# A decoder block on one core: cross-attention scores and feature map as two 64-row halves side by side, one more tile of cross weights, and new orders of work

## The reference, cut to what matters

```
v = values.reshape(N, -1, HEADS, HEAD_DIM)      # 16 heads of 16
v, k, q = (_feature_map(x, fm_w, fm_b) for x in (v, k, q))   # [exp(z), exp(-z)], z = x_h @ fm_w.T + fm_b: 32 features a head
scores = jnp.einsum('nqhd,nkhd->nhqk', q, k) / jnp.sqrt(jnp.float32(EMBED))
attn = jax.nn.softmax(scores, axis=-1)          # over 64 context rows
out = jnp.einsum('nhql,nlhd->nqhd', attn, v)
return out.reshape(N, S, HEADS * EXP_DIM) @ fc_w.T + fc_b
```

## Time and profile before

| | us |
|---|---|
| median of 3 runs (509.22, 513.79, 513.8) | 513.79 |
| profiled execution | 509.94 |
| its span | 508.0 |
| PE busy | 456.3 (90%) |
| DVE busy | 377.9 (74%) |
| ACT busy | 299.0 (59%) |
| POOL busy | 127.2 (25%) |

### The profile page before, as it was taken

The page is one execution under the profiler, slowest core; times in us unless marked ns, Lnnn a source line. Parts: engine busy times, 40 slices in busy tenths (PEclk is TensorE's granted clock), DMA queues, the critical chain, the costliest instruction groups (busy, mean ns, idle before and its releaser), DMA issues.

```text
span 508.0 us, 7573 instructions
## 1 busy us (share of the span) xinstructions
PE 456.3 (90%) x2424; PEld 289.7 (57%) x2424; DVE 377.9 (74%) x687; ACT 299.0 (59%) x727; POOL 127.2 (25%) x178
## 2 busy tenths in 40 slices
PE   1698879989799999999799999999799999977885
PEld 1463327446465676657365577656365676556664
DVE  5466676857589988667589988758599976657974
ACT  2457776665478846555468846555568846714531
POOL 2001113102413443013314343012414412112510
PEclk9889999999999999999889999999999999998999
DMA  8862500351610002232720002242621000000001
GB/s 276 280 203 72 180 0 1 93 154 45 224 67 1 0 3 76 73 122 64 249 82 1 2 2 62 74 120 77 217 73 37 8 3 0 21 22 0 2 1 43
DMA packets 22431, 38.46 MB, mean 76 GB/s; under 512 B 2552, under 2 KB 6904, under 8 KB 22264
## 3 DMA queue, kind: packets, MB, share of 16 engines
q1 hardware_dynamic: 22392, 37.97, 23.3%
HBM read 23.28 MB, written 14.68 MB: 75 GB/s over the span
## 4 chain that ended last, share of the span: by engine, by line
PE 69%; DVE 12%; issue 6%; ACT 5%; DMA 5%; SPq 2%; POOL 0%; POOLq 0%; ACTq 0%
PE av_bank L570 17%; PE m_bank L536 8%; PE m_bank L537 7%; PE m_bank L538 7%; PE s_pair L556 7%; PE m_bank L678 5%; DVE nmax L948 5%; DMA q_st<-q_parts 4%; ACT e_sb L770 3%; PE m_bank L703 2%; PE m_bank L690 2%; PE m_bank L739 2%; PE m_bank L587 2%; PE m_bank L728 2%; SPq L495 2%
## 5 line engine op out<-in xcount | busy, mean ns | idle before, releaser
L770 ACT ACTIVATE e_sb<-s_pair,nmax 128x512 f32<-128x512 f32 x256 | 173.1, 687 | 69.9 <-DVE nmax L948 69.6
L948 DVE TENSOR_REDUCE nmax<-s_pair 128x2 f32<-128x1024 f32 x128 | 152.4, 1212 | 27.1 <-PE s_pair L556 26.3
L570 PE MATMUL av_bank<-e_sb,v_sb 128*64 128x512 f32 x512 | 123.9, 604 | 3.4 <-DVE ot_lo L960 1.8
L1197 POOL TENSOR_TENSOR v_sb<-v_sb,rsum 128x256 f32<-128x256 f32 x64 | 39.2, 613 | 228.2 <-DVE rsum L956 218.2
L556 PE MATMUL s_pair<-q_st,k_st 64*128 64x512 f32 x256 | 51.1, 463 | 16.5 <-DMA q_st<-q_parts 9.6
L570 PEld LDWEIGHTS av_bank<-e_sb,v_sb 128*64 128x64 f32 x512 | 31.7, 136 | 57.7 <-issue 47.3
L556 PEld LDWEIGHTS s_pair<-q_st,k_st 64*128 64x128 f32 x256 | 21.3, 187 | 66.5 <-issue 31.1
L770 ACT ACTIVATION_READ_ACCUMULATOR e_sb<-s_pair,nmax 128x1 f32 x256 | 51.9, 203 | 0.0
L536 PE MATMUL m_bank<-wo_hi,ot_hi 128*128 128x256 f32 x120 | 35.0, 292 | 1.5 <-DVE ot_lo L960 1.5
L783 ACT ACTIVATE ot_hi<-av_bank 128x512 fp32r<-128x512 f32 x32 | 19.4, 605 | 27.9 <-PE m_bank L538 14.7
L1224 POOL TENSOR_TENSOR sx<-sx,xrec 128x512 f32<-128x512 f32 x24 | 24.9, 1043 | 36.5 <-DVE xrec L1121 36.5
(11 more groups left out here) (170 smaller groups left out, 869.6 us busy)
## 6 DMA issues: line engine op xcount, KB each, us to landing
q_st<-q_parts SPq DMA_DIRECT2D x32, 256.0 KB, 5.3
k_st<-k_parts SPq DMA_DIRECT2D x32, 256.0 KB, 4.4
k_parts<-qkt_hi SPq DMA_DIRECT2D x14, 256.0 KB
k_parts<-qkt_lo SPq DMA_DIRECT2D x14, 256.0 KB
q_parts<-qkt_hi SPq DMA_DIRECT2D x8, 256.0 KB
q_parts<-qkt_lo SPq DMA_DIRECT2D x8, 256.0 KB
out<-x_sb SPq DMA_DIRECT2D x8, 256.0 KB, 2.1
x_sb<-in_x SPq DMA_DIRECT2D x3, 512.0 KB, 7.7
```

Source lines behind the costliest of these rows:

```text
L570: mm = pe.matmul(av_bank[n % AV_BANKS][64 * par:64 * par + 64, :], v_sb[:, m, 2 * p + par, :], e_sb[:, (4 * q + 2 * i + par) % E_RING, :], ...
L770: act.activation(e_sb[:, g % E_RING, :], s_pair[k // 2][:, k % 2, :], ACT.Exp, bias=nmax[:, g % 8:g % 8 + 1], accum_out=esum[:, q % 4, k:k ...
L948: dve.tensor_reduce(nmax[:, at:at + 2], s_pair[i][:, :, :], AX_X, ALU.max, negate=True)\
L1197: pool.tensor_tensor(v_sb[:, m:m + 2, 2 * p:2 * p + 2, :], v_sb[:, m:m + 2, 2 * p:2 * p + 2, :], rsum[:, q % 4, :].rearrange("p (m h) -> p ...
```

## The change

`xs` and `z` become matmuls of 64 rows: the upper half of the partitions and the lower half each have their own matmul, their own weights and their own bank, alternating. An `xs` unit pair computes 8 such products of 128 columns instead of 4 of 128 rows x 256 columns; `z` computes 12 of 64 rows x 256 columns instead of 12 of 128 rows. Both halves of `xs` and `z` are one PE piece now, which waits for two banks. `kblk` shrinks to two blocks per group, and the heads' order in `vblk` and `wfc` follows. `sx` gets a fourth tile. All slots are laid out anew.

```diff
-X_TILES = 3
+X_TILES = 4
-    ("qk", 0, (1, 1), dict(pe=29, act=30, dve=43, sp=74)),
+    ("qk", 0, (1, 1), dict(pe=34, act=48, dve=39, sp=47)),
-    ("ld", 1, (2,), dict(sp=373)),
+    ("ld", 1, (2,), dict(sp=297)),
...
-    ("xs", -1, (0, 0), dict(pe=70, dve=71, act=69)),
+    ("xs", -1, (0, 0), dict(dve=68, act=69)),
+    ("xs", -1, (0,), dict(pe=57)),
...
-    ("kf", (1,), dict(pe=161, act=158)),
+    ("kf", (1,), dict(pe=-58, act=-77)),
-ATTENTION = dict(scores=3, weigh=34, max=(5, 6), exp=(5, 5, 9, 9), rsum=19, scale=16, ot_hi=30, ot_lo=38)
+ATTENTION = dict(scores=6, weigh=36, max=(6, 7), exp=(17, 18, 19, 19), rsum=22, scale=22, ot_hi=37, ot_lo=39)
...
-        kblk = sb("kblk", [P, 4, 4, L])
+        kblk = sb("kblk", [P, 4, 2, L])
...
-            def z(b, half, gg):
-                unit = ("z", b, (half, gg))
-                wait_bank(pe, unit)
...
-                for i in range(2):
-                    mm = matmul3(bank(unit)[:, i * HALF:(i + 1) * HALF], fm_hi[:, i], fm_lo[:, i],
-                                 xt2_hi[:, gg, :], xt2_lo[:, gg, :], True, True)
-                mm.then_inc(filled[uses[unit][0]], 1)
+            def z(b, half):
+                units = bank_units("z", b, (half,))
+                for unit in units:
+                    wait_bank(pe, unit)
...
+                for gg in range(DC):
+                    for k, (w, t) in enumerate(((fm_hi, xt2_hi), (fm_lo, xt2_hi), (fm_hi, xt2_lo))):
+                        for r, unit in enumerate(units):
+                            rows = slice(64 * r, 64 * r + 64)
+                            mm = pe.matmul(bank(unit)[:, gg * HALF:(gg + 1) * HALF], w[rows, r, :], t[rows, gg, :],
+                                           start=(k == 0), stop=(k == 2))
...
-                for i in range(2):
-                    mm = pe.matmul(bank(unit)[:, i * HALF:(i + 1) * HALF],
-                                   qf[:, 2 * gg + i, (t % 2) * P:(t % 2 + 1) * P],
-                                   kblk[:, 2 * gg + i].rearrange("p h l -> p (h l)"), start=True, stop=True)
-                mm.then_inc(filled[uses[unit][0]], 1)
+                for g in range(4):
+                    for r, unit in enumerate(units):
+                        rows = slice(64 * r, 64 * r + 64)
+                        mm = pe.matmul(bank(unit)[:, g * P:(g + 1) * P], qf[rows, g, (t % 2) * P:(t % 2 + 1) * P],
+                                       kblk[rows, g].rearrange("p h l -> p (h l)"), start=True, stop=True)
...
```

More of the change, by code:

```diff
@@ L134 @@
[L134 to L155, removed]
@@ L182 @@
+    ("fr", (1,), dict(pe=1990, act=1930)),
+    ("fv", (0,), dict(pe=1687, dve=1716, sp=1720)),
+    ("fr", (0,), dict(pe=1298, act=1328)),
+    ("fv", (1,), dict(pe=2296, dve=2289, sp=2295)),
 ]
 FIRST = [
[L185 to L198, removed]
-    ("ld", (1,), dict(sp=-25)),
-    ("ld", (2,), dict(sp=-24)),
-    ("v", (0, 2), dict(pe=-1, act=4)),
-    ("v", (0, 0), dict(pe=-35, act=3)),
@@ L203 @@
-    ("v", (0, 3), dict(pe=13, dve=18)),
+    ("cut", ("v",), dict(act=-222, dve=-57)),
+    ("load", ("fc",), dict(sp=-515)),
+    ("ln1", (0,), dict(dve=-1441, pool=-1103, do=-1097)),
+    ("t1", (0,), dict(dve=-723, pe=-586, act=-592)),
+    ("cut", ("qk",), dict(act=-881, dve=-864)),
+    ("ln1", (1,), dict(dve=-1119, pool=-860, do=-884)),
+    ("t1", (1,), dict(pe=-484, act=-515, dve=-487)),
+    ("qk", (0, 0), dict(dve=-452, sp=-464, pe=-459, act=-455)),
+    ("load", ("rest",), dict(sp=-927)),
@@ L204 @@
+    ("qk", (0, 1), dict(pe=-406, act=-420, dve=-440, sp=-403)),
+    ("load", ("o",), dict(sp=-989)),
+    ("ld", (0,), dict(sp=-375)),
+    ("load", ("feat",), dict(sp=-683)),
+    ("v", (0, 1), dict(pe=-4, dve=-13)),
+    ("ld", (1,), dict(sp=-325)),
+    ("ld", (2,), dict(sp=17)),
+    ("v", (0, 2), dict(pe=-4, act=12)),
+    ("v", (0, 0), dict(pe=-16, act=-16)),
+    ("v", (0, 3), dict(pe=19, dve=12)),
 ]
 ONCE = [
-    ("cut", ("o",), dict(act=-19, dve=-30)),
-    ("kf", (1,), dict(pe=161, act=158)),
@@ L246, in orders, with bank_units @@
     return {eng: sorted(units, key=lambda u: u[0]) for eng, units in out.items()}
+def bank_units(name, b, args):
+    if name in ("xs", "z"):
+        return [(name, b, args + (r,)) for r in range(2)]
+    return [(name, b, args)]
 def bank_uses(order):
@@ L257, in bank_uses @@
             ring = MISC_BANKS if 0 < scored < QUADS else MISC_BANKS + S_BANKS
-            uses[name, b, args] = (n % ring, had[n % ring])
-            had[n % ring] += 1
-            n += 1
+            for unit in bank_units(name, b, args):
+                uses[unit] = (n % ring, had[n % ring])
+                had[n % ring] += 1
+                n += 1
     return uses
@@ L266, in banks_before_scores @@
     first = [u[1] for u in order].index("scores")
-    units = [u[1:] for u in order[:first] if u[1] in BANKED]
+    units = [unit for u in order[:first] if u[1] in BANKED for unit in bank_units(*u[1:])]
     return [sum(uses[u][0] == MISC_BANKS + i for u in units) for i in range(S_BANKS)]
@@ L858, in t2, with z @@
                    .then_inc(xt2_hi_ready, 1)
-            def z(b, half, gg):
-                unit = ("z", b, (half, gg))
+            def z(b, half, r):
+                unit = ("z", b, (half, r))
                 wait_filled(act, unit)
@@ L865, in z @@
                     pb, ph = (b, 0) if half else (b - 1, 1)
-                    wait_filled(act, ("xs", pb, (2 * ph + 1, gg)))
-                act.activation(qf[:, 2 * gg:2 * gg + 2, :], bank(unit)[:, :].rearrange("p (g n) -> p g n", g=2),
+                    for rows in range(2):
+                        wait_filled(act, ("xs", pb, (2 * ph + 1, rows)))
+                act.activation(qf[:, :, :].rearrange("p (g r) n -> p r g n", r=2)[:, r], bank(unit)[:, :].rearrange("p (g n) -> p g n", g=2),
                                ACT.Exp, bias=fmb[:, 0:1]).then_inc(emptied[uses[unit][0]], 1)
@@ L1260 @@
         "fm_b": np.asarray(L0_xattn_fm_b).reshape(KD, 1),
-        "wfc": rows(np.asarray(L0_xattn_fc_w).T, 4),
+        "wfc": rows(wfc, 4),
         "fc_b": np.asarray(L0_xattn_fc_b),
```

276 lines of the change are left out of this document (157 added, 119 removed).

## The result

The changed kernel takes **489.6 us** (median of four runs, 484.82 to 491.64). The kernel before took 512.35 us beside it (four runs, 509.22 to 513.8). The ratio is 0.957, with a 95% interval of 0.951 to 0.962: faster by 22.8 us.

What follows compares the result with a forecast made beforehand. PE was taken to set the pace, except for waits for `q_st` and a stretch where VectorE is full too. Terms −8 − 15.8 + 0 − 1 − 2 + 3 = −23.8 from 509.94 gave 486 us, range 477 to 502.

Steps and rivals of the forecast that it cites:

- The load: Fifth quads of elements 1 to 3: issuing pair 2's load earlier removes PE's waits and the low clock behind, −15.8 us.
- Packing under the quads: `xs` and `z` under later quads of three elements: 64-row matmuls side by side save PE work, −8 us (0 to −11.6).
- The price of the work: PE work saved by packing `xs` and `z`, less changes of form: 3.9 us per element, 11.6 for three.
- the discount for the stretch in which VectorE is full as well: Element 0's `xs` stretch, 146 to 186 us: VectorE is full too, so −8 us was taken instead of −11.6.
- The predicted 0.87 us per tile: `xs` on PE: 16 passes, two side by side, in 8 slots of 0.11 us, against 1.73 us before.
- The rule weighed in the prediction: `xs` pairs on PE: weight loads overlap matmuls only when row groups differ, so a slot would be load plus matmul.
- Two banks at once: `z` and `xs` waiting for two of three banks: a quarter microsecond per `xs`, +3 us (0 to 33).
- slower: Rival, chance 0.06: PE is held at two banks by a full VectorE, 2.7 us at each of 12 `xs`; 526 us.
- Element 0's own quads: Element 0's quads, 78.6 us before: `kf` 1 leaves the tenth quad, −1 us (−2 to 0).
- The tail: After the last scores, 67.8 us before: PE loses 3.7 us of work, half on the path, −2 us (−3.7 to +1.5).
- Packing gives nothing: Rival, chance 0.20: weight loads stand ahead of each pair, or VectorE keeps the stretch at its length; 500 us.
- The wait for a stack moves: Rival, chance 0.12: another of the eight pairs, for instance pair 0, is short by 3 us instead; 502 us.

Runs made afterwards that it cites:

- early load (1): Kernel before with one slot changed: SP issues the load of pair 2 ahead of the writes of the keys' half 1; 495.09 us, ratio 0.967.
- experiment 3: Changed kernel with packing undone for `z` and `xs` (matmuls over all 128 rows), same banks, tiles and orders; 501.66 us, ratio 0.983.
- experiment 8: Orders of the kernel before with the load of pair 2 early, plus packed code, joined pieces and four tiles, few slots moved; 525.93 us, ratio 1.032.
- experiment 2: Changed kernel with the load of pair 2 put back behind the writes of the keys' half 1; 499.45 us, ratio 0.976.
- Experiment 4: Changed kernel with packing undone for `xs` alone, `z` still packed; 496.28 us, ratio 0.970 over three runs; a fourth took 503.36 us.
- experiment 5: Changed kernel with ACT turning the second half's `z` into `qf` ahead of two exponentials in the tail; 489.0 us, ratio 0.956.
- experiment 7: Changed kernel with two tiles for the feature map `qf`, one per half of the rows; 488.97 us, ratio 0.957.
- experiment 9: Changed kernel with 55 extra transposes of the identity keeping PE busy at three places in the tail; 486.86 us, ratio 0.954.
- experiment 11: Changed kernel with three tail edits together: extra PE transposes spread anew, ACT's `z` piece earlier, two `qf` tiles; 488.69 us, ratio 0.954.

## Why the prediction was right, and which steps were off

The stretches of four profiled executions, in us, tell the parts apart. Each column adds one part to the one left of it; the tail includes what follows the last quad's first scores.

| stretch | before | early load (1) | and new orders, two banks, 4 tiles (3) | and packed (the change) |
|---|---|---|---|---|
| start | 32.2 | 32.4 | 31.3 | 32.0 |
| element 0's quads | 78.6 | 79.4 | 79.0 | 83.3 |
| element 1 | 113.6 | 109.1 | 109.1 | 105.4 |
| element 2 | 115.1 | 109.0 | 109.3 | 105.4 |
| element 3 | 100.7 | 95.9 | 96.0 | 92.1 |
| tail | 67.8 | 67.7 | 75.1 | 71.4 |

**The load: −15.8 forecast, −15.4 measured** within the three elements. The mechanism, the places and the low clock behind them were as read.

**Packing under the quads: −8 forecast, −11.5 measured** (3.7 + 3.9 + 3.9). The price of the work was right, 3.9 us per element. What failed is the discount for the stretch in which VectorE is full as well. The whole amount came off the path. One reservation: experiment 3 is not the old `xs`. It has pieces of 128 columns, 2.02 us per tile, of which sixteen passes of 0.112 are 1.79 and the rest is change of form; the 256 columns of before took 2 x 0.87 = 1.74 without one. The forecast's sum goes from column 2 to column 4, and there the gain is 3.7, 3.6 and 3.8 us, 11.1 in all. The predicted 0.87 us per tile came out as 1.11 with its change of form.

**Halves side by side.** Two `xs` passes of 64 rows take the 0.11 us of one over all rows (0.112 in experiment 3). The rule weighed in the prediction (the Trainium skill, *TensorE: Matmul & The Clock Gate*, Part 3, The mechanism) would have made it load plus matmul in turn, with nothing saved. The trace disagrees: pairs follow each other every 0.112 us, and so do the passes of experiment 3, which all use the same rows and load weights each time.

**Two banks at once: +3 forecast, 0 measured** in the new orders: no wait at L679 or L696 between 116 and 418 us. In the old orders it was no small term. The time of the *slower* rival (526 us, chance 0.06) turned up in experiment 8, 525.9 us, mostly by another road. At the joined pieces PE waited 10.7 us for ACT's `qf` and only 0.3 for VectorE. VectorE held it for 13.3 us, but at other pieces: 6.1 at `weigh`, 5.7 at `pt` and 1.5 at `pv`. What kept the changed kernel from that is the new layout of the orders, whose merit I had not priced; which of its slots do it was not tested.

**Element 0's own quads: −1 forecast, +4.7 measured.** This step failed, for two reasons. The same orders ran there in experiments 2 to 5, 7, 9 and 11. Where the clock was full throughout, but for what reaches over quad 16, they took 80.2, 79.0 and 80.1 us (experiments 2, 3 and 5), 0.4 to 1.6 more than before and not 1 less: the −1 for moving `kf` out did not show. PE waits longer at quad 16 (2.77 us, and 2.3 to 3.4 in experiments 2, 3 and 5, against 1.9 before) for stacks whose keys SP writes at 103.65; `kf` by itself was not tested. The rest is clock. With one, two, three and four stretches of 3.4 us at half clock the same quads took 80.9, 81.9, 83.3 and 85.0 us (experiments 9, 7, the changed kernel and 11), about 1.2 us for each. Experiment 4, also with four, took 84.6. The row of experiment 11:

```profile
31.80:116.80 85.00, 73.74 (x312) 34.68 (x312) 54.48 (x81) 54.37 (x146) 13.36 (x22) 0.92 0.28 86
```

What brings those stretches stays open. The same piece of the program, first in the changed kernel, then in experiment 5, ahead of the first stretch and in it:

```profile
32.00:37.70 5.70, 3.92 (x17) 2.25 (x18) 5.07 (x7) 3.71 (x10) 0.61 (x1) 1.00 0.48 159
37.70:41.10 3.40, 3.40 (x9) 1.50 (x9) 1.54 (x3) 2.79 (x8) 0.06 (x1) 0.50 0.48 149
```

```profile
31.20:36.90 5.70, 3.87 (x17) 2.26 (x18) 5.00 (x7) 2.82 (x9) 0.61 (x1) 1.00 0.47 153
36.90:40.30 3.40, 3.40 (x17) 1.38 (x15) 1.55 (x4) 2.79 (x8) 0.07 (x1) 1.00 0.48 149
```

PE was idle for 1.8 us of the 5.7 ahead in both, in waits of under 0.9 us. One execution got 0.50 behind it and the other 1.00. Idle PE stands ahead of the low clock in the places looked at, but the profile does not tell when it comes. It also goes with the spread of the runs: the four of the changed kernel, 491.64, 489.82, 489.37 and 484.82 us, have mean granted clocks of 0.964, 0.967, 0.971 and 0.984.

**The tail: −2 forecast, +3.6 measured.** The saved work was worth more than I took: 75.1 to 71.4, the upper bound of 3.7. That amount is not clean, since the clock differs (10.2 us low before it, 13.6 behind). But the new layout of the tail costs 7.4 us (67.7 to 75.1), which I had costed at nothing, having read only what the packing takes from it. Layout means new slots and joined pieces on two banks, and the two were never taken apart: with the old slots and joined pieces, experiment 8's tail took 76.2 us, so the slots alone need not be the cause. Part of the 7.4 us is clock: 13.6 us of it are low in the changed kernel and 3.4 before, and keeping PE busy gave back 1.6. Another part is in waits that hand over to each other (`qf`, then POOL's `e_sb`: experiments 5, 7, 11), worth 1.2 more when all were taken away together. About 0.8 us is left unexplained, and a little more since experiment 11 has no low clock there at all and the kernel before has 3.4 us.

**The rivals.** *Packing gives nothing* fell by experiment 3. *The wait for a stack moves* fell in the main: the three waits are gone, and only the one at quad 16 grew, by 0.9 us (by 0.4 to 1.5 in experiments 2, 3 and 5). That the whole came within 4 us of the forecast owes something to misses that cancel: 3.5 and 3 us too little gain under the quads, 5.7 and 5.6 us too much at the two ends. Part of the closeness is the choice of execution, too: the sum starts from one profiled at 509.94 us, under its kernel's median, and from that one to the changed kernel's profiled 491.64 us the gain is 18.3 us and not 23.8.

## What to carry to other kernels

Read a change stretch by stretch, and price the new order of each stretch as well as the new work: here the new layout cost 7 us in the tail, while in the old orders, fitted in the one way that was tried, the packing made the kernel 31 us slower. When an engine waits for data with another transfer ahead in the same queue, count the low clock behind the wait too, and try the one-line move first. A saving on an engine that was busy for 97% of a stretch came off the path in full here, although a second engine was full for a third of it, but only once the orders kept the first engine from waiting.

## What the hardware showed

- Matmuls of 64 rows on the two halves of the array overlap in fp32 with a weight load for every 128 columns: 0.112 us per pair of passes, each with its own weights, as much as one pass over all rows. For `xs`, 2.02 us became 1.11.
- A change of the array's form cost as much as before, 0.15 to 0.2 us each. The Trainium skill, *TensorEngine Tiling (Array Packing)*, Key Properties, says that it drains the engine; the runs show the price and not the drain by itself. 22 more of them were worth their price.
- TensorE's clock fell to 1.2 GHz (0.50) in stretches of mostly 3.4 or 6.8 us, in the places looked at with idle time of PE ahead, of 2 to 3 us in one piece or of under 1 us in several. The same instructions on PE with nearly the same idle time ahead (1.78 and 1.83 of 5.70 us) got either level in two executions.
